# VectorE loads the next count row's two bases behind the row's first addition instead of at its end

## The reference

```python
def rgcn_conv(x, edge_index, edge_type, W_rel, W_root, bias):
    N = x.shape[0]
    src, dst = (edge_index[0], edge_index[1])
    h_src = x[src]
    out = x @ W_root + bias
    for r in range(NUM_REL):
        w = (edge_type == r).astype(x.dtype)
        msg = h_src @ W_rel[r] * w[:, None]
        sums = jax.ops.segment_sum(msg, dst, num_segments=N)
        cnt = jax.ops.segment_sum(w, dst, num_segments=N)
        out = out + sums / jnp.maximum(cnt, 1.0)[:, None]
    return out
...
x = _layernorm(x + L0(x))      # the relational network above, ELU, a projection back to 1024
x = _layernorm(x + L1(x))      # three layers of h + MLP(h + segment_sum(h[src], dst)), decoder
```

## Time and profile before

| | us |
|---|---|
| median of 3 runs | 574.75 (574.73 to 575.24) |
| the profiled execution | 576.75 |
| its span, first to last instruction | 574.9 |
| PE busy | 556.9 (97%) |
| DVE busy | 371.8 (65%) |
| ACT busy | 243.5 (42%) |
| POOL busy | 101.7 (18%) |
| granted TensorE clock, mean | 0.992 |

### The profile page before, as it was taken

The page is one execution under the profiler, slowest core; times in us unless marked ns, Lnnn a source line. Parts: engine busy times, 40 slices in busy tenths (PEclk is TensorE's granted clock), DMA queues, the critical chain, the costliest instruction groups (busy, mean ns, idle before and its releaser), DMA issues.

```text
span 574.9 us, 8853 instructions
## 1 busy us (share of the span) xinstructions
PE 556.9 (97%) x2708; PEld 399.4 (69%) x2708; DVE 371.8 (65%) x1070; ACT 243.5 (42%) x484; POOL 101.7 (18%) x80
## 2 busy tenths in 40 slices
PE   6999999999999999999999999999999999999992
PEld 3655555555588989888889888868868867555541
DVE  7588898888838889887430230048658667855555
ACT  3363465636565464653222121023232233366555
POOL 4010000000000000020444532202202230132230
PEclk8999999999999999999999999999999999999998
DMA  8511011111031211238200001500100100022123
GB/s 265 151 31 27 22 36 36 36 36 36 2 93 37 72 38 45 64 102 231 112 2 0 0 0 29 201 1 1 38 0 0 37 0 2 0 73 65 42 72 107
DMA packets 20963, 30.77 MB, mean 54 GB/s; under 512 B 5458, under 2 KB 15404, under 8 KB 20928
## 3 DMA queue, kind: packets, MB, share of 16 engines
q1 hardware_dynamic: 20512, 29.66, 17.4%
q10 hardware_dynamic: 416, 0.67, 0.4%
HBM read 25.20 MB, written 5.12 MB: 53 GB/s over the span
## 4 chain that ended last, share of the span: by engine, by line
PE 77%; DVE 9%; DVEq 5%; issue 5%; DMA 2%; ACT 1%; POOL 0%; SPq 0%
PE banks L991 12%; PE banks L1077 12%; PE banks L906 12%; PE banks L781 8%; PE banks L874 5%; PE banks L1013 5%; PE banks L1003 4%; PE banks L939 4%; PE banks L941 4%; DVEq L1253 3%; PE banks L1067 3%; DVE cnt L1261 2%; PE banks L916 2%; DVE oh_both L1241 2%; DVE oh_both L1236 1%
## 5 line engine op out<-in xcount | busy, mean ns | idle before, releaser
L781 PE MATMUL banks<-w_all,xnT 128*125 128x429 f32 x320 | 133.4, 541 | 2.5 <-DMA w_all<-in_L_gnn_W_rel 2.5
L781 PEld LDWEIGHTS banks<-w_all,xnT 128*125 128x125 f32 x320 | 54.6, 190 | 32.6 <-issue 32.6
L906 PE MATMUL banks<-hT,w_s 128*128 128x250 f32 x320 | 68.9, 375 | 0.1
L906 PEld LDWEIGHTS banks<-hT,w_s 128*128 128x128 f32 x320 | 60.2, 189 | 8.5 <-issue 1.4
L939 PE MATMUL banks<-y_hi,adj 125*125 125x288 f32 x200 | 55.2, 303 | 0.3 <-issue 0.3
L1261 DVE TENSOR_TENSOR cnt<-cnt,banks 125x110 f32 x160 | 42.6, 266 | 18.1 <-issue 12.6
L941 PE MATMUL banks<-y_lo,adj 125*125 125x286 f32 x200 | 53.5, 294 | 0.0
L991 PE MATMUL banks<-adj,h_hi 125*128 125x250 f32 (+1 forms) x180 | 48.3, 367 | 0.3 <-issue 0.2
L1408 DVE TENSOR_SCALAR hT<-banks,g_c,b_c 128x125 f32<-128x125 f32 x60 | 19.4, 401 | 45.1 <-PE banks L891 45.0
L759 PEld LDWEIGHTS banks<-oh_both,oh_low 125*128 125x128 bf16 x320 | 23.2, 98 | 34.9 <-issue 20.1
L991 PE MATMUL banks<-adj,h_lo 125*128 125x250 f32 (+1 forms) x180 | 45.7, 353 | 0.0
(11 more groups left out here) (224 smaller groups left out, 943.5 us busy)
## 6 DMA issues: line engine op xcount, KB each, us to landing
xt<-in_x SPq DMA_DIRECT2D x15, 448.0 KB
out_x<-ot SPq DMA_DIRECT2D x9, 448.0 KB
w_s<-in_L_gnn_W SPq DMA_DIRECT2D x5, 512.0 KB, 6.4
xn<-in_x SPq DMA_DIRECT2D x5, 448.0 KB
wd_s<-in_L_gnn_Wd SPq DMA_DIRECT2D x1, 2048.0 KB, 11.9
w_all<-in_L_gnn_W_rel SPq DMA_DIRECT2D x6, 286.0 KB, 6.6
wo_s<-in_L_gnn_wo_weight SPq DMA_DIRECT2D x1, 1024.0 KB, 6.2
w_all<-in_L_gnn_W_root SPq DMA_DIRECT2D x3, 286.0 KB, 5.9
```

The lines of the kernel that those rows point to most:

```text
L781: ins = pe.matmul(pb[0:P, 2 + 2 * v + n, 0:FH], xnT[:, u], w_all[:, u, n * FH:(n + 1) * FH], start=(u == 0), stop=(u == KD - 1))
L906: ins = pe.matmul(pb[:, b0 if f == 0 else 4 + f % 2, 0:2 * P], w1_s[:, k, f * 128:(f + 1) * 128], hT[:, k], start=(k == 0), stop=(k == KD ...
```

## The change

The load of the next row's bases is issued behind the first addition of the current row, ahead of the next codes, and no longer at the row's end. The second addition keeps the current row's registers (`now`). No instruction is added or removed; the tile's first load (at the tile's start) and the last row of a tile, which has no load, are as they were. 8 rows in each of tiles 1 to 8 and 7 rows of tile 9 are concerned.

```diff
                     dve.wait_ge(counts_mm, g + 1)
                     dve.wait_ge(counts_free, g + 2)
                     place(base, b, 0, placed, first_added)
+                    now = base
+                    if u + 1 < rows:
+                        base = bases(g + 1)
                     more = rows == UG or u + 2 < rows
                     if more:
                         codes(g + 2, b).then_inc(codes_set, 1)
                         lows(g + 2, b)
                     dve.wait_ge(first_added, g + 1)
-                    place(base, b, 1, placed, counts_free)
+                    place(now, b, 1, placed, counts_free)
                     if more:
                         weighed_codes(g + 2, b).then_inc(onehots, 1)
-                    if u + 1 < rows:
-                        base = bases(g + 1)
```

## The result

The changed kernel takes 598.76 us (median of 4 runs, 598.28 to 599.82) against 575.0 us before (574.73 to 577.76): a ratio of 1.0402, with a 95% interval of 1.0379 to 1.0425. The forecast was 597.0 in a range of 591.5 to 602.0. The direction, the size and the main mechanism came out as forecast. A delay of PE behind the phase was not in it: 1.4 us where it arises, 0.6 us at the end of the span. The median grew by 23.8 us, the span of the two profiles, counted from the first addition of the phase, by 23.4; the 0.4 us between them lie within the spread of the single runs.

A forecast was written before the change was run, and what follows sets the result against it. DVE's row, 1.91 us against PE's 1.71, was to bound the whole count phase; 64 longer rows and tile 9 end it 22.3 us later, so 574.75 + 22.3 = 597.05, given as 597.0 us, range 591.5 to 602.0.

The forecast's parts named there:

- The sequencer issues nothing during a load: On DVE, the sequencer works in order, so no other operation is issued during a load's 0.53 us.
- the reciprocal's step behind the load: On DVE, the reciprocal uses no base register, yet its register step comes 0.03 us behind the load's end.
- Rivals 1 and 2: 1: load runs beside the codes, 573.0 us, chance 0.06; 2: exposed part stays 0.26 us, 574.75 to 578, chance 0.03.
- 0.26 us of exposure at the row's end: In a DVE row before the change, the load costs 0.26 us; the rest of it is hidden.
- Codes at +0.82 and a row of 1.91 us: In the changed DVE row, codes start at +0.82 instead of +0.19 us; the row takes 1.91 instead of 1.56 us.
- 64 rows, 22.1 us until tile 9: Tiles 1 to 8: 64 rows at +0.35 us make 22.4 us, 22.1 after an earlier DVE wait covers 0.35.
- the meetings with POOL: POOL's subtraction holds up DVE once a tile; change over eight tiles -4.5 to +4 us, taken as nothing.
- Tile 9: Begins on DVE at 168.9 us, rows of 1.78 us; the projection ends at 182.0 instead of 159.75.
- Everything behind it is not touched.: Behind the projection's end, bias load and aggregation only shift, so the whole kernel gets 22.3 us longer.
- The span for the median: The profiled span of 574.9 us may stand for the median of 574.75, to which 22.3 us is added.
- rival 3: PE's clock falls to the 1.2 GHz level as PE waits in each row; up to 90 us, chance 0.02.

The follow-up runs named there:

- e3: The kernel before the change, with the load moved from the row's end to between codes and lows in all rows: 587.17 us, ratio 1.0199.
- e10: The changed kernel with four values loaded each time instead of two, the last two unused: 608.59 us, ratio 1.0549 against the kernel before the change.
- e1: The kernel before the change without the 71 loads of bases inside a tile, so counts land in other columns: 571.74 us, ratio 0.9945.
- e2: The kernel before the change, with the load moved from the row's end to behind codes and lows, ahead of the second addition: 574.60 us, ratio 0.9985.
- e4: The kernel before the change, with the load moved from the row's end to behind the second addition, ahead of the weighed codes: 575.16 us, ratio 0.9999.
- e9: The kernel before the change, with two rows' bases (four values) per load at the row's end, each pair beginning at an even row: 573.22 us, ratio 0.9931.
- e7: The kernel before the change, with two rows' bases (four values) loaded at once at the end of every second row: 573.07 us, ratio 0.9959.

## Why the prediction was right, point by point

- **The sequencer issues nothing during a load.** Right: in no profile does a record of DVE's sequencer start within one of these loads, e3 and e10 show idle time ahead of operations that need none of the loaded registers, and tile 9 shows it with no register step between. The forecast's own proof, the reciprocal's step behind the load, was weaker than it was said to be: that is a register step too, so it showed only that the sequencer's steps wait. Rivals 1 and 2 fall.
- **0.26 us of exposure at the row's end.** Right: the row without a load takes 1.29 us (e1).
- **Codes at +0.82 and a row of 1.91 us.** 0.80 and 1.92; in most tiles five of the eight loaded rows take 1.91 or 1.92, and the others are those beside the reciprocal and the one that meets POOL.
- **64 rows, 22.1 us until tile 9.** 22.45. It is luck that it came so close, since two small terms cancelled that were not in the sum: the meetings with POOL cost some 1.4 us more than before in eight tiles (0.76 us a tile in the mean instead of 0.59, up to 1.04), and the two rows around the reciprocal took 3.83 us together, where the sum had 0.70 more than the 3.32 (odd tiles) or 3.24 (even tiles) of before, some 1.2 us less over eight tiles.
- **Tile 9.** I had +0.2 us to the projection's end; it was +0.3, but not in the way forecast. DVE was to set the pace with 1.78 us a row. Its rows took 1.70, as the codes started 0.59 us behind the first addition, and that is no more than PE's 1.71, so PE was the bound again from 170 us on. The meeting with POOL cost 1.03 us instead of 0.7, and the two misses nearly cancelled.
- **"Everything behind it is not touched."** This is the step that failed. PE's sequencer does not wait for the projection's end to go on; it goes on when its last count row is free, and has 3.3 us of branch to spend. In the profile of before the last products covered all of it but 0.15 us, and the change takes 1.4 us of this cover. After what the bias load covers, it cost about 0.6 us of the 23.4. An operation that is not in the busy time of any engine stood on the second-longest path.
- **The span for the median.** The profiled run of before took 576.75 us and its span 574.9, so 1.85 us lie around a span; the other runs must have had spans nearer 573. I set the span equal to the median of other, shorter runs. That did no harm, since only the difference was used, but the profiled run had begun its phase later than some runs do, as below.
- **The clock.** It stayed at 1.00 with PE busy for 90% of the stage; rival 3 falls.

## What to carry to other kernels

A load into registers costs its engine the load's length less the data work that the sequencer has already handed over. So it belongs behind the longest run of operations that need no wait, with as few register steps as possible between it and the next operation (e2 against e4); putting it "earlier" can take its cover away. Ask of each move what is queued at that moment on that engine, and, of each engine that becomes late, which sequencer work of its partners (a branch, a load) was hidden behind it. Loading at once what several steps need was worth more here (0.7% in e9) than the best place for a load of two values (0.15% in e2).

## What the runs showed of the hardware

A TENSOR_LOAD of four 4-byte values by DVE's sequencer took 0.34 to 0.38 us when they began at an even row (median 0.344 in e9), 0.96 to 0.98 us at an odd row; in e10 the two lengths alternate over all 80 loads. Two values took 0.52 to 0.56 us wherever they began. Neither expectation for e7 had four values take less time than two.

PE's branch behind the ninth tile took 3.3 to 3.8 us in all thirteen profiles, and the aggregation never started before its end.

The first addition came between 23.5 and 26.4 us in the profiles, with the same program ahead of it. So single profiles of this kernel differ by up to 3 us for a reason that has nothing to do with a change to the count rows; its cause was not looked for.
